# Re-timing the head of a graph kernel's build: casts moved to GpSimd, list work moved between steps, first sums begun earlier

## What is computed

```python
h = relu(layernorm(x));  x = x + hypergraph_conv(h)   # two means over neighbours, twice, W1, W2
h = relu(layernorm(x));  x = x + relational_gru(h)    # h[src] + relvec[rel], summed by dst, a GRU cell
h = relu(layernorm(x));  x = x + gcn(h)               # W, normalised sum over edges, layer norm, relu
h = relu(layernorm(x));  x = x + attention(h)         # softmax over 4 heads of each edge
```

## Time and profile before

| | |
|---|---|
| median of 3 runs | 1184.93 us (1182.42 to 1186.74) |
| the profiled execution | 1172.69 us, span 1171.1 us |
| TensorE busy | 1075.0 us, 92% of the span |
| VectorE busy | 705.4 us, 60% |
| ScalarE busy | 400.5 us, 34% |
| GpSimd busy | 350.7 us, 30% |
| sums of the first mean (L2410) | 625, 187.9 us |
| waits of VectorE for products (L2224 on L2460) from 55 to 270 us | 16.0 us in 23 |

### The profile page before, as it was taken

How to read it: one execution, slowest core, us unless ns; L and a number is a source line. 1 busy time by engine, 2 the same in 40 slices (tenths; PEclk the granted TensorE clock), 3 DMA queues, 4 the chain that set the end, 5 groups by cost and what they waited for, 6 DMA issues and landing times.

```text
span 1171.1 us, 21528 instructions
## 1 busy us (share of the span) xinstructions
PE 1075.0 (92%) x8207; PEld 828.9 (71%) x8207; DVE 705.4 (60%) x2239; ACT 400.5 (34%) x878; POOL 350.7 (30%) x502
## 2 busy tenths in 40 slices
PE   0799999989999997999999999999999998999980
PEld 0466666668887873667888888676667677888960
DVE  7998878964546563521455552365546665867776
ACT  3866665437654510211112211222222222221123
POOL 7421120120000025653111112675556110455110
PEclk9999999999999997999999999999999999999985
DMA  5210010047897714433455543343334221222103
GB/s 183 84 48 20 19 27 20 15 73 194 186 195 185 178 47 154 113 104 109 160 195 162 169 137 109 100 134 97 101 106 124 84 75 50 56 67 58 29 6 112
DMA packets 114282, 119.55 MB, mean 102 GB/s; under 512 B 55033, under 2 KB 92804, under 8 KB 114159
## 3 DMA queue, kind: packets, MB, share of 16 engines
q1 hardware_dynamic: 94876, 77.60, 24.2%
q0 software_dynamic: 12032, 27.45, 8.4%
q10 hardware_dynamic: 7262, 13.04, 3.3%
HBM read 65.33 MB, written 35.50 MB: 86 GB/s over the span
## 4 chain that ended last, share of the span: by engine, by line
PE 77%; DVE 14%; issue 3%; POOL 2%; ACT 1%; DMA 1%; SPq 0%; POOLq 0%; DVEq 0%; ACTq 0%
PE ps L632 21%; PE ps L590 16%; PE ps L1068 9%; PE ps L2410 8%; PE ps L1037 4%; PE ps L1171 3%; PE ps L1173 3%; PE ps L2452 2%; PE ps L1096 2%; PE ps L1177 2%; PE ps L1175 2%; PE ps L1197 2%; PE ps L1081 1%; PE ps L1224 1%; DMA adj<-in_dst_rows,adj 1%
## 5 line engine op out<-in xcount | busy, mean ns | idle before, releaser
L632 PE MATMUL ps<-big,pairB 128*128 128x250 fp8e4 (+1 forms) x2600 | 279.9, 268 | 5.4 <-issue 3.4
L632 PEld LDWEIGHTS ps<-big,pairB 128*128 128x128 f16 x2600 | 246.6, 98 | 37.8 <-issue 5.5
L2410 PE MATMUL ps<-pairA,adj 125*125 125x512 f16 x625 | 187.9, 383 | 0.2 <-ACT adj L2339 0.2
L944 POOL TENSOR_TENSOR st<-st,mhalf 125x1 f32<-125x1 f32 x76 | 52.0, 684 | 320.6 <-DVE st L1706 320.3
L590 PE MATMUL ps<-adj,pairB 125*128 125x250 fp8e4 (+1 forms) x1300 | 140.0, 267 | 1.2 <-DVE pairB L1768 1.2
L590 PEld LDWEIGHTS ps<-adj,pairB 125*128 125x128 f16 x1300 | 122.8, 98 | 17.0 <-DVE pairB L1768 1.5
L2339 ACT ACTIVATE adj<-ps 125x450 fp8e4<-125x450 f32 (+6 forms) x191 | 98.2, 520 | 77.3 <-PE ps L2452 64.4
L1068 PE MATMUL ps<-pairA,adj 125*125 125x512 f16 x450 | 103.4, 388 | 8.6 <-issue 8.3
L2410 PEld LDWEIGHTS ps<-pairA,adj 125*125 125x125 fp8e4 x625 | 78.6, 138 | 38.0 <-issue 1.4
L1068 PEld LDWEIGHTS ps<-pairA,adj 125*125 125x125 fp8e4 x450 | 62.6, 140 | 47.4 <-issue 13.5
L590 PE MATMUL ps<-adj,pairA 125*128 125x250 fp8e4 (+1 forms) x800 | 84.0, 264 | 1.1 <-issue 1.0
(11 more groups left out here) (371 smaller groups left out, 1824.8 us busy)
## 6 DMA issues: line engine op xcount, KB each, us to landing
t_adjTp<-big SPq DMA_DIRECT2D x25, 416.0 KB, 3.8
big<-t_adjTp ACTq DMA_DIRECT2D x25, 416.0 KB
pairB<-xin SPq DMA_DIRECT2D x100, 64.0 KB, 2.0
t_pairs<-pairA SPq DMA_DIRECT2D x50, 112.0 KB
t_xh<-work SPq DMA_DIRECT2D x13, 256.0 KB
pairB<-in_x SPq DMA_DIRECT2D x5, 640.0 KB, 9.8
t_h0p<-pairB SPq DMA_DIRECT2D x5, 640.0 KB
work<-t_xh SPq DMA_DIRECT2D x25, 128.0 KB
```

Source lines behind the costliest of these rows:

```text
L632: last = pe.matmul(out, half_pair(k, m, b)[:, FEAT * part + 128 * c:FEAT * part + 128 * (c + 1)], slots[:, s:s + n, m, 0:P, b], start=star ...
L944: g.tensor_tensor(st[:, 9:10], st[:, 8:9], k.mhalf[:, 0:1], ALU.pow).then_inc(S[rstd], 1)
L2410: last = pe.matmul(k.ps[0:P, 6 + t % 2, :], k.adj[:, j, PITCH * i:PITCH * i + P], k.pairA[:, j, :], start=(j == 0), stop=(j == TILES - 1))
```

## The change

Six things move, all in `build`.

1. **Sums earlier.** `SUMMED` gets ten sums ahead, one more behind each slot from 17 to 26 (two behind slot 18, by the rounding); the lead then falls evenly to none at the last slot.
2. **Casts to GpSimd.** The high halves of tiles 15 to 24 are cast by GpSimd, behind its list work and ahead of the fetches of chunks; `low_of` of the last two groups waits for these.
3. **Placing in steps.** The lists of groups 1 to 5 are placed one by one at slots 10, 12, 14, 16 and 18, where all five stood at slot 8.
4. **List work later.** In VectorE's loop `chunks` goes from step 3 to 4 (behind `low_of(3)`), `starts` from 5 and 7 to 7 and 9, `keys` from 9 on to 10 on, the words from 14, 18, 22, 26 to 15, 19, 23, 27, and the first three transposes of keys by eight slots.
5. **Bounds later.** `magnitudes` goes from step 4 to 6, `scales` from 6 to 10, `bounds` from slot 40 to 64; they use other buffers.
6. **`h0p`** is written when the tiles are normalised, not when their high halves are copied.

As sums end earlier and the inverse degrees stay in their steps, the steps of scaling and combining move too.

```diff
-TURNS = (*(80 + BULK * g for g in range(GROUPS - 1)), 128)
+TURNS = (*(88 + BULK * g for g in range(GROUPS - 1)), 128)
+LEAD, LEAD_FROM, HI_ACT = 10, 17, 15
 ...
-        out.append(min(TILES * sum(stop + 5 <= s for stop in STOP), round(upto)))
+        ahead = min(LEAD, max(0, s - LEAD_FROM + 1)) * (SLOTS - 1 - s) / (SLOTS - 1 - LEAD_FROM)
+        out.append(max(out[-1] if out else 0, min(TILES * sum(stop + 5 <= s for stop in STOP), round(upto + ahead))))
 ...
-    WORDS = (14, 18, 22, 26)
+    WORDS = (15, 19, 23, 27)
 ...
-            sp.wait_ge(h_ready, per * (n + 1))
+            sp.wait_ge(h_own, per * (n + 1))
 ...
         root(4)
+        for i in range(HI_ACT, TILES):
+            pool.wait_ge(h_own, i + 1)
+            g.tensor_copy(k.pairA[:, i, 0:FEAT], k.xall[:, i, :]).then_inc(tabled, 1)
         for n in range(1, ALL):
             gather_near(n)
 ...
         def low_of(n):
-            dve.wait_ge(h_ready, per * (n + 1))
+            if per * n < HI_ACT:
+                dve.wait_ge(h_ready, per * (n + 1))
+            else:
+                dve.wait_ge(tabled, 4 + per * (n + 1) - HI_ACT)
 ...
-            dve.wait_ge(placed, 1 if a == 0 else 2)
+            dve.wait_ge(placed, b)
 ...
-            stt(out=mag, in0=k.W1[:, :, :], scalar=-1.0, in1=k.W1[:, :, :], op0=ALU.mult, op1=ALU.max).then_inc(abs_ready, 1)
+            for c in range(KC):
+                stt(out=k.extra_all[c][:, :], in0=k.W1[:, c, :], scalar=-1.0, in1=k.W1[:, c, :], op0=ALU.mult, op1=ALU.max
+                    ).then_inc(abs_ready, 1)
 ...
-            if m == 3:
-                chunks(1, ALL)
             if m == 1 or m == 2:
                 low_of(m)
             if 4 <= m <= BATCH:
                 low_of(m - 1)
             if m == 4:
+                chunks(1, ALL)
+            if m == 6:
                 magnitudes()
-            if m == 5:
+            if m == 7:
                 starts(1, GROUPS)
-            if m == 6:
+            if m == 9:
+                starts(GROUPS, ALL)
+            if m == 10:
                 scales()
                 v.memset(k.odeg8[:, :], 0.0)
-            if m == 7:
-                starts(GROUPS, ALL)
-            if 9 <= m < 9 + ALL - 1:
-                keys(m - 8, m - 7)
+            if 10 <= m < 10 + ALL - 1:
+                keys(m - 9, m - 8)
 ...
-            if i > 2 * per:
+            if 2 * per < i <= HI_ACT:
                 act.wait_ge(h_own, i)
                 s.activation(k.pairA[:, i - 1, 0:FEAT], k.xall[:, i - 1, :], ACT.Copy).then_inc(h_ready, 1)
 ...
+        PLACES = tuple(range(BULK + 2, BULK + 2 + 2 * (ALL - 1), 2))
 ...
-            if s == BULK:
-                place(1, ALL)
-            if s == 5 * BULK:
+            if s in PLACES:
+                place(1 + PLACES.index(s), 2 + PLACES.index(s))
+            if s == 8 * BULK:
                 bounds()
```

More of the change, by code:

```diff
@@ L2151, in magnitudes @@
         def magnitudes():
-            scratch, mag = k.st[1], k.work[:, 0:2 * FEAT].rearrange("f (c n) -> f c n", c=KC)
-            absb = k.t[0]
+            scratch, absb = k.st[1], k.b2
             dve.wait_ge(small_in, 48)
-            stt(out=mag, in0=k.W1[:, :, :], scalar=-1.0, in1=k.W1[:, :, :], op0=ALU.mult, op1=ALU.max).then_inc(abs_ready, 1)
+            for c in range(KC):
+                stt(out=k.extra_all[c][:, :], in0=k.W1[:, c, :], scalar=-1.0, in1=k.W1[:, c, :], op0=ALU.mult, op1=ALU.max
+                    ).then_inc(abs_ready, 1)
             stt(out=absb, in0=k.b1[:, :], scalar=-1.0, in1=k.b1[:, :], op0=ALU.mult, op1=ALU.max)
@@ L2161, in scales @@
         def scales():
-            scratch, absb = k.st[1], k.t[0]
+            scratch, absb = k.st[1], k.b2
             dve.wait_ge(bound, 1)
@@ L2382, in scalar @@
                 n += 1
-            if m % 2 == 1 and m < 2 * (3 * per + 1):
+            if m % 2 == 1 and m < 2 * (3 * per):
                 h_of(2 * per + m // 2)
@@ L2479, in bounds @@
         def bounds():
-            pe.wait_ge(abs_ready, 1)
-            mag = k.work[:, 0:2 * FEAT].rearrange("f (c n) -> f c n", c=KC)
+            pe.wait_ge(abs_ready, KC)
             for c in range(KC):
-                last = pe.matmul(k.ps[0:P, 3, 0:FEAT], k.ones[:, :], mag[:, c, :], start=(c == 0), stop=(c == KC - 1))
+                last = pe.matmul(k.ps[0:P, 3, 0:FEAT], k.ones[:, :], k.extra_all[c][:, :], start=(c == 0), stop=(c == KC - 1))
             last.then_inc(bound, 1)
+        PLACES = tuple(range(BULK + 2, BULK + 2 + 2 * (ALL - 1), 2))
         place(0, 1)
```

## The result

The changed kernel takes **1193.71 us** (median of 5 runs, 1190.32 to 1198.17) beside 1184.68 us for the kernel before (median of 5 runs, 1182.42 to 1186.74): ratio **1.0082**, 95% interval 1.0059 to 1.0104. That is 9.0 us slower, where 1.2 us was forecast, and above the range of 1181.2 to 1190.1. The profiled execution of the changed kernel took 1192.18 us (span 1190.1).

A forecast was written before the change was run, and what follows sets the result against it. VectorE and TensorE, in step, were taken to bound the build by turns. TensorE's lead, -0.9 after product 14, then -0.4 - 0.65 + 0.71, gave -1.2: 1184.93 + 1.2 = 1186.1 us, range 1181.2 to 1190.1.

The forecast's parts named there:

- Up to the 21st sum: Build head: low halves at 53.35, 21st sum at 53.5 behind a TensorE wait of 0 to 4 us; lead 1.45.
- The stall of 0.9 before mask 2: VectorE, ready at 43.6, waits for product 2 at 44.3, delayed by six sums and a placing step; 0.9 (0 to 2.4).
- ScalarE being late for nobody here: Build head: the reason given why taking ScalarE's copies over to GpSimd changes nothing; costed at nothing.
- Up to product 8: TensorE dense, lead 2.0; product 8 at 71.85 with 80 sums, VectorE waiting some 2.8 us before mask 8.
- Costed at nothing: Items given no cost: two absolute values, placing in five steps, SyncE's earlier writes of normalised tiles, GpSimd's chunk fetches behind casts.
- The casts: Ten GpSimd casts each cost VectorE 0 to 0.47 us, 0 to 4.7 in all; 0.7 taken.
- the rival of the casts: Casts collide with VectorE each time, 4.7 instead of 0.7 us between 38 and 53 us; 1190.1 us, chance 0.15.
- Products 8 to 14: VectorE's list work and pairs heap up, 29.2 us against 26.3 before; 2.9 us lost, lead falls to -0.9.
- such a pair: Inverse degree and combine in one VectorE step, waiting 0.59 while ScalarE scales; 1.34 us each, three make 4.0.
- The load: VectorE's work from mask 8 to mask 13 sums to 28.7 us; TensorE waits about 4, mostly before product 14.
- To the end: TensorE dense to slot 440: 0.4 lost, 0.65 of sums not cashed, 0.71 wait gone; build ends 1.2 us later.
- the clock rival: TensorE falls back to the 1.2 GHz level in the new wait, lead 1.5 to 2 lower; 1188.0 us, chance 0.22.

The follow-up runs named there:

- E5: Changed kernel with inverse degrees at the head of VectorE's step, all casts back on ScalarE and the late h0p write; ratio to the kernel before 0.9998.
- E10: Changed kernel with the late h0p write and inverse degrees at the head of VectorE's step, casts kept on GpSimd; product 76 at 249.09 us.
- E9: Changed kernel with one line changed, the first 15 normalised tiles written only when their half-precision copies are there; product 76 at 257.56 us.
- E7: Kernel before with one line changed, the early write of the normalised tiles alone; mask 0 at 39.54, product 76 at 251.29 us.
- E3: Kernel before with the ten early sums alone; product 76 at 256.52 us, ratio to the kernel before 1.0061.
- E8: Kernel before, unchanged, run again for its trace; product 76 at 249.59 us.

## Why the prediction was wrong, step by step

- **Up to the 21st sum: right in the result, by other terms.** Low halves of tiles 20 to 24 at 52.33 + 1.48 = 53.81 (VectorE's last row below), foretold 53.35; the wait was 1.75, foretold 0 to 4. The stall of 0.9 before mask 2 isn't in the changed kernel (VectorE has no idle time over 0.4 us there). In its place stand a late start that was not foretold (mask 0 at 39.53 for 38.56, 0.97) and the casts (1.05): 51.75 + 0.97 + 1.05 = 53.77. That the sum came near is partly luck. In E5, with no late start and no casts, the stall shows, at 0.99:

```profile
44.37 0.24 DVE L2233 TENSOR_TENSOR wih<-ps,wih 128x80 bf16<-128x80 f32 x1 [0.99 <-PE ps L2470]
```

  "ScalarE being late for nobody here" was a wrong reading: before 49 us TensorE waits nine times for evictions in the kernel before, 4.7 us in all. It cost the forecast nothing that shows; product 8 comes at 70.53 with the casts on GpSimd (E10) and at 70.66 without (E5).
- **Up to product 8: right by luck.** 71.89 with 80 sums, foretold 71.85; VectorE idle 2.23 before mask 8, foretold 2.8 (the items of that sum add up to 16.0, where it has 15.8). Without the early write the same chain stands at 70.81 (E9) or 70.53 (E10), so the forecast was 1.0 to 1.3 us too slow and the early write hid it. The first step that failed: "Costed at nothing: ... SyncE's writes of the normalised tiles, which wait for less than before". Waiting for less means starting sooner, here while the first edges were being fetched; alone it cost 1.70 us (E7).
- **The casts: 1.05 against 0.7.** The rows of the changed kernel (VectorE, then GpSimd) show how they meet VectorE:

```profile
39.68 1.67 DVE L2116 TENSOR_TENSOR pairA<-pairB,pairA 125x1280 f16<-125x1280 f32 x1
...
42.58 0.48 DVE L2220 TENSOR_TENSOR wih<-big,work 128x256 bf16<-128x256 f16 x1
...
45.77 1.48 DVE L2116 TENSOR_TENSOR pairA<-pairB,pairA 125x1280 f16<-125x1280 f32 x1
...
52.33 1.48 DVE L2116 TENSOR_TENSOR pairA<-pairB,pairA 125x1280 f16<-125x1280 f32 x1
```

```profile
39.61 0.39 POOL L2075 CAST pairA<-pairB 125x256 f16<-125x256 f32 x1
...
39.96 1.65 POOL L2075 CAST pairA<-pairB 125x256 f16<-125x256 f32 x1
...
46.02 1.49 POOL L2075 CAST pairA<-pairB 125x256 f16<-125x256 f32 x1 [0.83 <-ACT pairB L2328]
...
48.64 0.40 POOL L2075 CAST pairA<-pairB 125x256 f16<-125x256 f32 x1 [0.75 <-ACT pairB L2328]
```

  Five VectorE instructions between 39.6 and 45.6 us are longer by 0.19 to 0.22 each than in E5, which has no casts, and a sixth by 0.05. The casts pay more: 0.40 us alone, 1.65 and 1.49 beside a low half, and they end 0.26 us after it (41.35 and 41.61, 47.25 and 47.51); the cast behind the first of them starts at 41.55. The Trainium skill, "SBUF — State Buffer", section "SBUF: two separate sides", has one of the two block for the other's whole instruction; the trace agrees, with the cast as the one that mostly waits. So the rival of the casts had the meeting right and its payer wrong: VectorE lost about 0.2 us in each of five instructions, not 0.47 in each of ten.
- **Products 8 to 14: here it failed.** The prediction put "such a pair" of inverse degree and combine at 1.34 us on VectorE, from the one pair of the earlier trace rows, and counted of its waiting only VectorE's 0.59. That wait came true (0.59 in the row of 77.41). But the pair has a third member, the scale on ScalarE between the two. The prediction asked of TensorE's new wait what is queued behind it; of the scale it didn't ask. The sign was in the trace of before, on ScalarE, where the scales of turns 0 and 2 already wait for their inverses, with evictions queued behind them:

```profile
61.23 0.47 ACT L2356 ACTIVATE work<-ps,rsB 125x256 f32<-125x256 f32 x1 [2.98 <-DVE rsB L2232]
...
75.12 0.47 ACT L2356 ACTIVATE work<-ps,rsB 125x256 f32<-125x256 f32 x1 [1.66 <-issue]
```

  TensorE loses 0.17 us at the first of them and nothing at the second. Ten sums earlier, the scale of turn 0 waits 5.08 us in E3 and that of turn 2 waits 5.58 in the changed kernel, and TensorE stops. The term was 0; by E10 it was 5.64 between products 8 and 9, of which 3.79 are the stop and the remaining 1.85 the slow sums behind it.
- **The load: the right place, half the size.** Without the stop, product 14 comes 27.75 us after product 8 (E10), foretold 29.2; the kernel before takes 26.32. So the load costs 1.4 us, not 2.9. TensorE's wait there is one of 2.60 before product 14 for mask 13, foretold about 4, "mostly before product 14". E10 has the inverses at the head of the step, so a part of the difference may be theirs.
- **To the end: about right.** From product 14 to product 76 the sum has 150.1 us; 150.73 were measured in the changed kernel and 150.81 in E10. With the two missed steps out of the way, E10 ends 0.50 us before E8, where the prediction had 1.2 us after.
- **The rivals.** Slow sums were there, but not where the clock rival had them: behind the new wait of 1.75 us at 53.87 the pairs take 0.59 to 0.62; behind the stop of 3.79, which no case had, they take 1.06. The price, 1.5 to 2 there and 1.85 here, agrees by luck. The Trainium skill, "TensorE: Matmul & The Clock Gate", section "HAM oscillation — how this bites in real kernels", says that a wait can throttle the array and slow the next burst; the rows of 77.88 and 78.95 agree. The fast rival had product 14 at 96.5; it came at 106.11, and with the stop gone at 98.28.

## What to carry to other kernels

When a producer is moved earlier, follow its result to the next engine and look at what stands behind the consumer in that engine's queue: a small instruction that waits there holds everything behind it. Put short instructions that others wait for (an inverse, a flag, a copy) at the head of a step, ahead of long work, where a wait for their own input can come out of one that is there anyway, as the 1.15 us in E10 did. A wait that is made weaker starts its transfer sooner, so it has a price too: look for the transfer that it now meets.

## What the hardware showed that was not expected

- With a write of 640 KB issued 1.36 us earlier, a small gather took 4.3 to 4.4 us instead of 3.1 to 3.3, in every trace of the five kernels that have it (first mask 39.53 to 39.58).
- Where a GpSimd cast met a VectorE instruction with two operands in SBUF, the cast waited for its end (1.65 and 1.49 us for 0.40).
- Two executions of one build agree within 0.4 us at 250 us, while the stretch from 715 to 910 us differs by some 8 us between one chip and two others (202.1 to 204.1 and 193.2 to 196.1).
- Waits of 2.60 and 2.61 us at the same place left TensorE at full spacing once and at half once.
